# Attention weights times v in 64x64 blocks, with one transpose ahead of them, and a later wait for m

## The chip, the cores and the metric

The kernel runs on one core of one Trainium2 chip. The metric is the device time of one execution in microseconds (us). Engines: TensorE (matmuls, "PE" in the profile, its weight loads "PEld"), VectorE ("DVE"), ScalarE ("ACT"), GpSimd ("POOL") and SyncE ("SP", DMA issues only).

## The reference

One transformer block with adaptive layer norms, for 8 batch rows of 2048 tokens and 256 channels, in 32-bit floats. The attention is linear in the tokens: its scores are a 64x64 matrix per head, from q and k summed over all tokens.

```python
mod = (silu(c) @ wmod)                      # sa, ca, ga, sb, cb, gb of each batch row
h = layernorm(x) * (1 + ca) + sa
q, k, v = split(h @ w_qkv + b_qkv)          # 8 heads of 64
scores = einsum('bhld,bhle->bhde', q, k) / 8
attn = softmax(scores)                      # 64x64 per head
out = einsum('bhld,bhde->bhle', v, attn)
out = layernorm(out @ w_fc + b_fc + h) * gamma + beta
x = x + ga * out
h = layernorm(x) * (1 + cb) + sb            # then a gated FFN on h and h shifted by a token:
x = x + gb * sigmoid(xr @ W_r.T) * (relu(xk @ W_k.T) ** 2 @ W_v.T)
```

## The kernel before

The kernel handles one batch row after another, and each row in four chunks of 512 tokens. It doesn't form q, k and v of the tokens. With z the normalised x of a row (256 channels), it sums the Gram matrix z'z over the row (`turn_and_gram`), puts the weights on both sides of it (`gram_q`, `scores`), takes the softmax of eight 64x64 matrices, and folds attention, the v weights and the output weights into one 256x256 matrix m (`wv_attn`, `make_m`). The attention of a chunk is then z times m (`attention`). Then come the second norm, whose result z2 is transposed (`turn_z2`), and the FFN (`ffn_r`, `ffn_k`, `ffn_out`).

The order of the work is written out by hand, for every engine on its own, and the engines meet in semaphores. `row_steps(b)` of TensorE does the attention and FFN of row b and, between them, the preparation of m for row n = b + 1. It is called for row 0, then by a loop over rows 1 to 6; row 7 has `last_row`, which holds no preparation. So the preparation of m is in seven turns, and once in the start (`wv_attn(0)` and `make_m(0)`), after the constants and weights have been prepared.

The names and lines that matter:

- `wv_attn` (lines 1474 to 1481): four matmuls, one for a pair p of heads. The stationary operand is `attn[:, p]`, 128x128, with the two heads' 64x64 matrices on its diagonal and zeros elsewhere (GpSimd clears it once). The moving operand is `wv_aug[:, p]`, 128 x 256, the v weights. Pairs 0 and 1 go to the PSUM bank att[0], pairs 2 and 3 to att[1]; each bank signals `pv_done` when full. It waits for `attn_ready` (VectorE, line 1087) and `wv_ready` (VectorE, line 1063; in the start GpSimd, line 509).
- ScalarE copies the two banks to SBUF (`copy_pv`, line 642), in two halves, each of which signals `pv_ready`. The copy shares its buffer with gq, so the profile calls it `gq<-att`.
- `make_m` (lines 1483 to 1489): eight matmuls of 256 columns, for each half k of the channels one for each pair p, into the bank gram. It waits for both copies. VectorE then turns the result into m in a high and a low part (lines 1094 to 1099), for which `attention` of the next row waits. In the start `fc_ready` is waited for as well.
- `turn_z2(b, 3)` (lines 1379 to 1393): eight 128x128 transposes of z2 of chunk 3, between `wv_attn` and `make_m`. They wait for z2 (ScalarE, line 717) and for free banks tr. ScalarE's `copy_h2` (line 661) reads them.
- `scores` (lines 1463 to 1472): sixteen matmuls with 128 rows and 64 columns of the stationary operand, head g of a pair in column half g, into partitions 64g to 64g + 63 of the bank gram.
- around them on TensorE, in order: `ffn_out(b, 1)`, `scores(n)`, `ffn_r(b, 2)` (line 1408), `ffn_k(b, 2)` (line 1425), `wv_attn(n)`, `turn_z2(b, 3)`, `make_m(n)`, `ffn_out(b, 2)` (lines 1239 to 1241), then `attention(b + 1, 0)` (the same lines).

Of the kernel before, what the change touches and what calls it, by code (L numbers as in the profile page):

```python
# [30 lines left out]
P = 128  # L31


def adaln_block(nc, x, w_qkv, b_qkv, w_fc, b_fc, gamma, beta, w_r, w_k, w_v, mu_r, mu_k, c, wmod, out):
    B, L, D = x.shape
    HD = w_fc.shape[0]
    DX = 64
    H = HD // DX
    KD = D // P
    NP = H // 2  # L40
    CT = 512
    CH = L // CT
    NT = CT // P
# [10 lines left out]
    with ExitStack() as ctx:  # L54
        def sb(name, shape):
            return ctx.enter_context(nc.sbuf_tensor(name, shape, F32))
# [4 lines left out]
        def bank(name):  # L61
            return ctx.enter_context(nc.psum_tensor(name, [P, 512], F32))

        def sem(name):
            return ctx.enter_context(nc.semaphore(name))
# [3 lines left out]
        tr = [bank(f"tr{h}") for h in range(KD)]  # L69
        att = [bank(f"att{q}") for q in range(2)]  # L70
        work = [bank(f"work{w}") for w in range(3)]

        def r_banks(alone):

            return (att[0], att[1]) if alone else (work[2], work[0])
# [9 lines left out]
        ident = sb("ident", [P, P])  # L85
# [33 lines left out]
        wv_aug = sb("wv_aug", [P, NP, D])  # L119
# [8 lines left out]
        attn = sb("attn", [P, NP, P])  # L128
# [22 lines left out]
        z2 = sb("z2", [P, NT, D])  # L151
# [22 lines left out]
        def mixed(j):  # L174

            return xr[:, j % 2], xk[:, j % 2]
# [58 lines left out]
        wv_ready = sem("wv_ready")  # L235
# [9 lines left out]
        attn_ready = sem("attn_ready")  # L245
        pv_done = sem("pv_done")
        pv_ready = sem("pv_ready")
# [26 lines left out]
        z2_ready = sem("z2_ready")  # L274
        z2_turned = sem("z2_turned")
        h2_ready = sem("h2_ready")
# [20 lines left out]
        def wait_past(eng, semaphore, count):  # L297

            if not isinstance(count, int) or count > 0:
                eng.wait_ge(semaphore, count)  # L300
# [932 lines left out]
        def _(pe):  # L1233
            mm = nc.tensor.matmul
# [87 lines left out]
            def turn_ffn():  # L1322

                pe.wait_ge(ffn_loaded, 48)
                pe.wait_ge(z_lo_ready, 2 * CH)
                pe.wait_ge(row8_b_ready, 1)
                for n, bank in enumerate((tr[0], tr[1], work[0])):
                    for ch in range(KD):
                        for dh in range(KD):
                            ins = nc.tensor.transpose(bank[:, ch * D + dh * P:ch * D + (dh + 1) * P],  # L1330
                                                      w_ffn[:, n, dh, ch * P:(ch + 1) * P], ident[:])
                    ins.then_inc(w_turned, 1)
# [27 lines left out]
            def attention(b, j, alone=False):  # L1360
                i = CH * b + j
                pe.wait_ge(m_ready, b + 1)
                pe.wait_ge(z_lo_ready, 2 * i + 2)
                if not alone:
                    wait_past(pe, t_done, i)
                elif j == 1:
                    pe.wait_ge(h2_ready, 2 * CH * b)
                else:
                    pe.wait_ge(t_done, i - (j == 2))
                for q in range(2):  # L1370
                    for t in (2 * q, 2 * q + 1):
                        tile = slice(t * P, (t + 1) * P)
                        for k in range(KD):
                            ins = mm3(att_banks(j, alone)[q][:, (t % 2) * D:(t % 2 + 1) * D],
                                      (z_hi[:, j, k, tile], z_lo[:, j, k, tile], m_hi[:, k], m_lo[:, k]),
                                      start=(k == 0), stop=(k == KD - 1))
                    ins.then_inc(att_done, 1)

            def turn_z2(b, j, last=False):
                i = CH * b + j  # L1380
                pe.wait_ge(z2_ready, i + 1)


                if last and j == 0:
                    pe.wait_ge(t_done, CH * b + 2)
                elif last or j == CH - 1:
                    wait_past(pe, h2_ready, 2 * i)
                for h in range(KD):
                    if not last and j < CH - 1:
                        pe.wait_ge(z_lo_ready, 2 * (i + 1 + CH) + 1 + h)  # L1390
                    for t in range(NT):
                        ins = nc.tensor.transpose(tr[h][:, t * P:(t + 1) * P], z2[:, t, h * P:(h + 1) * P], ident[:])  # L1392
                    ins.then_inc(z2_turned, 1)

            def ffn_r(b, j, alone=False):

                i = CH * b + j
                pe.wait_ge(xr_mixed, i + 1)
                for q in range(2):
                    if alone:  # L1400
                        pe.wait_ge(t_done, CH * (b + 1))
                        pe.wait_ge(th_ready, 2 * i - 1 + q)
                    elif q == 1:
                        wait_past(pe, ro_ready, 2 * i - 1)
                    for t in (2 * q, 2 * q + 1):
                        tile = slice(t * P, (t + 1) * P)
                        for ch in range(KD):
                            ins = mm(r_banks(alone)[q][:, (t % 2) * D:(t % 2 + 1) * D], mixed(j)[0][:, ch, tile], w_r_t[:, ch],  # L1408
                                     start=(ch == 0), stop=(ch == KD - 1))
                    ins.then_inc(r_done, 1)  # L1410

            def ffn_k(b, j, alone=False):

                i = CH * b + j
                pe.wait_ge(xk_mixed, i + 1)
                for dh in range(KD):
                    if dh == 0 and not alone:
                        wait_past(pe, ro_ready, 2 * i)
                    elif not alone:
                        pe.wait_ge(th_ready, 2 * i + 1)  # L1420
                    elif j == CH - 1:
                        pe.wait_ge(k_lo_ready, 2 * i - 1 + dh)
                    rows_dh = slice(dh * P, (dh + 1) * P)
                    for ch in range(KD):
                        ins = mm(k_banks(alone)[dh][:], w_k_t[:, ch, rows_dh], mixed(j)[1][:, ch],  # L1425
                                 start=(ch == 0), stop=(ch == KD - 1))
                    ins.then_inc(k_done, 1)
# [19 lines left out]
            def turn_gram(b):  # L1447

                pe.wait_ge(g_up_ready, b + 1)
                nc.tensor.transpose(gram[:, D + P:2 * D], g_sb[:, 0, P:D], ident[:]).then_inc(gram_turned, 1)  # L1450
# [21 lines left out]
                ins.then_inc(score_done, 1)  # L1472

            def wv_attn(b):

                pe.wait_ge(attn_ready, b + 1)
                pe.wait_ge(wv_ready, b + 1)
                for p in range(NP):
                    ins = mm(att[p // 2][:, (p % 2) * D:(p % 2 + 1) * D], attn[:, p], wv_aug[:, p], start=True, stop=True)  # L1479
                    if p % 2:  # L1480
                        ins.then_inc(pv_done, 1)

            def make_m(b):

                pe.wait_ge(pv_ready, 2 * b + 2)
                for k in range(KD):
                    for p in range(NP):
                        ins = mm(gram[:, k * D:(k + 1) * D], pv_t[:, p, k * P:(k + 1) * P], wfc_c[:, p], start=(p == 0), stop=(p == NP - 1))  # L1488
                ins.then_inc(m_done, 1)

            def row_steps(b, first):

                n = b + 1
                attention(b, 0)
                turn_and_gram(n, 0)
                if not first:
                    ffn_r(b - 1, 3)
                    ffn_k(b - 1, 3)
                attention(b, 1)
                if not first:  # L1500
                    ffn_out(b - 1, 3)
                turn_and_gram(n, 1)
                turn_z2(b, 0)
                attention(b, 2)
                turn_and_gram(n, 2)
                ffn_r(b, 0)
                ffn_k(b, 0)
                turn_z2(b, 1)
                attention(b, 3)
                ffn_out(b, 0)  # L1510
                turn_and_gram(n, 3)
                turn_z2(b, 2)
                turn_gram(n)
                ffn_r(b, 1)
                ffn_k(b, 1)
                gram_q(n)
                ffn_out(b, 1)
                scores(n)
                ffn_r(b, 2)
                ffn_k(b, 2)  # L1520
                wv_attn(n)
                turn_z2(b, 3)
                make_m(n)
                ffn_out(b, 2)

# [38 lines left out]
            bias_v()  # L1564
            mod_b_columns()
            turn_ffn()
            wv_attn(0)
            pe.wait_ge(fc_ready, 1)
            make_m(0)
            pe.wait_ge(w_copied, 5)  # L1570
            row_steps(0, True)
# [27 lines left out]
```

## Time and profile before

| | us |
|---|---|
| median of 3 runs | 679.94 (679.27 to 681.49) |
| the profiled execution | 681.61 |
| its span | 679.8 |
| TensorE busy | 654.6 |
| VectorE busy | 567.8 |
| ScalarE busy | 457.0 |
| GpSimd busy | 294.0 |
| mean granted clock of TensorE | 0.991 of full |

The profile is of one execution. The span runs from the first instruction to the last; the execution's own time is 1.8 us longer. Matmuls are pipelined and their ends are modelled, so a matmul row's duration is longer than its share of the engine: the distance from one start to the next tells what it costs. A group "x8" lasts from the first start to the last modelled end. "L1479" is line 1479 of the kernel before. A 32-bit matmul appears as two weight loads and two matmul records, here called passes; a transpose appears as one.

### The profile page before, as it was taken

The page shows a single profiled execution, that of the slowest core. Times are in us where ns is not written, and L with a number is a line of the kernel's source. Part 1 is how long each engine was busy: PE and PEld are TensorE (multiplying, and loading weights), DVE is VectorE, ACT ScalarE, POOL GpSimd, SP SyncE. Part 2 cuts the span into 40 slices and gives each one's busy share as a digit, 9 for nine tenths or more (in the row PEclk, how much of TensorE's full clock was granted, in tenths as well). Part 3 has the DMA queues.
Part 4 walks back from the last instruction along what each step waited for, and adds up shares of the span by engine and source line. Part 5 has one row for each costly group of instructions (what it writes and reads, how often), then busy time and mean ns, then how long its engine had stood idle before and what let it go on. Part 6 is the DMA issues. An engine that isn't in the chain of part 4 may idle for free.

```text
span 679.8 us, 12488 instructions
## 1 busy us (share of the span) xinstructions
PE 654.6 (96%) x3968; PEld 535.5 (79%) x3968; DVE 567.8 (84%) x1328; ACT 457.0 (67%) x983; POOL 294.0 (43%) x499
## 2 busy tenths in 40 slices
PE   8978799999999999999999999999999999999896
PEld 6657777889869887889878888798878888697665
DVE  5893988889798897889888897889888897859973
ACT  1423767676966779667867769577776769667662
POOL 5263452764318442574227542383327643215230
PEclk9988999999999999999999999999999999999999
DMA  8859237384854958086765758268673737537325
GB/s 315 224 166 198 89 113 160 61 182 123 195 111 83 230 109 208 31 167 165 162 123 100 170 125 204 79 108 224 129 156 62 128 84 169 101 76 154 63 32 92
DMA packets 90985, 93.04 MB, mean 137 GB/s; under 512 B 4224, under 2 KB 89000, under 8 KB 90960
## 3 DMA queue, kind: packets, MB, share of 16 engines
q0 software_dynamic: 33264, 33.03, 32.9%
q1 hardware_dynamic: 55344, 55.97, 26.1%
q10 hardware_dynamic: 2352, 3.73, 1.5%
q8 instruction: 12, 0.20, 0.1%
q14 instruction: 13, 0.11, 0.0%
HBM read 42.84 MB, written 33.10 MB: 112 GB/s over the span
## 4 chain that ended last, share of the span: by engine, by line
PE 85%; DVE 7%; POOL 2%; ACT 2%; DMA 2%; issue 2%; DVEq 0%; POOLq 0%; ACTq 0%
PE work L1408 14%; PE work L1425 14%; PE gram L1355 10%; PE att L1239 4%; PE work L1239 4%; PE gram L1488 4%; PE work L1240 4%; PE work L1241 4%; PE att L1241 4%; PE att L1240 4%; PE tr L1392 4%; PE att L1460 4%; PE tr L1348 3%; PE att L1479 2%; PE gram L1470 1%
## 5 line engine op out<-in xcount | busy, mean ns | idle before, releaser
L478 POOL TENSOR_TENSOR rs<-ve,neg_half 128x4 f32<-128x4 f32 x32 | 37.4, 1170 | 179.3 <-DVE ve L945 179.3
L1425 PE MATMUL work<-mx,w_k_t 128*128 128x512 f32 x244 | 109.9, 592 | 0.0
L1408 PE MATMUL work<-w_r_t,mx 128*128 128x256 f32 x464 | 106.0, 381 | 0.3 <-DVE mx L983 0.3
L717 ACT ACTIVATE z<-x,nm,rs 128x256 f32<-128x256 f32 x128 | 66.4, 594 | 46.5 <-POOL nm L480 46.5
L1408 PEld LDWEIGHTS work<-w_r_t,mx 128*128 128x128 f32 x464 | 85.8, 190 | 11.8 <-DVE mx L983 0.5
L1355 PE MATMUL gram<-z 128*128 128x256 f32 (+1 forms) x512 | 89.1, 327 | 0.0
L1355 PEld LDWEIGHTS gram<-z 128*128 128x128 f32 x512 | 79.8, 191 | 6.6
L1425 PEld LDWEIGHTS work<-mx,w_k_t 128*128 128x128 f32 x244 | 46.3, 190 | 46.0 <-issue 42.4
L1239 PE MATMUL att<-m_lo,z_hi 128*128 128x256 f32 x248 | 74.9, 302 | 3.8 <-issue 2.0
L1239 PE MATMUL work<-wvf_lo,k_hi 128*128 128x256 f32 x248 | 72.0, 290 | 2.5 <-issue 2.5
L1240 PE MATMUL att<-m_hi,z_hi 128*128 128x256 f32 x248 | 70.8, 285 | 0.0
L1241 PE MATMUL att<-m_hi,z_lo 128*128 128x256 f32 x248 | 70.7, 285 | 0.0
L1241 PE MATMUL work<-wvf_hi,k_lo 128*128 128x256 f32 x248 | 69.1, 279 | 0.0
L1240 PE MATMUL work<-wvf_hi,k_hi 128*128 128x256 f32 x248 | 69.1, 278 | 0.0
L652 ACT ACTIVATE sq<-att 128x256 f32<-128x256 f32 x124 | 45.7, 381 | 33.1 <-PE att L1241 33.1
L924 DVE SCALAR_TENSOR_TENSOR t_buf<-att,rs_o,g_row 128x256 f32<-128x256 f32 x124 | 51.4, 477 | 10.7 <-POOL rs_o L487 9.9
L485 POOL TENSOR_TENSOR ve_o<-ssq,eps_att 128x4 f32<-128x4 f32 x32 | 17.0, 531 | 94.0 <-ACT sq L652 94.0
L661 ACT ACTIVATE h2t<-tr,mod_now 128x512 f32<-128x512 f32 x64 | 46.4, 781 | 15.2 <-PE tr L1392 15.2
L1000 DVE TENSOR_TENSOR k_lo<-work,k_hi 128x512 fp32r<-128x512 f32 x60 | 40.6, 689 | 18.7 <-ACT k_hi L702 18.5
L492 POOL DMA_DIRECT2D x<-in_L_attn_x_dram x32 | 55.2, 1823 | 0.0
L957 DVE SCALAR_TENSOR_TENSOR mx<-h2t,rest_col,mx 128x512 f32<-128x512 f32 x56 | 39.4, 745 | 17.5 <-ACT mx L670 17.5
L1239 PEld LDWEIGHTS att<-m_lo,z_hi 128*128 128x128 f32 x248 | 48.0, 193 | 7.5 <-issue 7.5
(186 smaller groups left out, 1633.1 us busy)
## 6 DMA issues: line engine op xcount, KB each, us to landing
x_in<-in_L_attn_x_dram SPq DMA_DIRECT2D x32, 512.0 KB, 5.1
x<-rows SPq DMA_DIRECT2D x32, 512.0 KB, 3.5
x<-in_L_attn_x_dram POOLq DMA_DIRECT2D x32, 512.0 KB, 8.7
out_dram<-x SPq DMA_DIRECT2D x31, 512.0 KB, 5.3
out_dram<-y POOLq DMA_DIRECT2D x29, 512.0 KB, 5.9
rows<-row_scratch SPq DMA_DIRECT2D x16, 128.0 KB, 5.0
rows<-row_scratch SPq DMA_DIRECT2D x8, 256.0 KB, 4.0
wqkv_sb<-in_L_attn_w_qkv_dram ACTq DMA_DIRECT2D x1, 1536.0 KB, 9.5
```

Of the source, the lines that this page charges most:

```text
L492: nc.gpsimd.dma_start(x2[:, j], x_v[b, j], accum_op=ALU.add).then_inc(x2_filled[j], 16)
L652: ins = nc.scalar.activation(sq[:, t], att_banks(j, alone)[t // 2][:, (t % 2) * D:(t % 2 + 1) * D], ACT.Square, scale=float(D) ** -0.5, ac ...
L661: nc.scalar.activation(h2t[:, h, 1 + j * CT:1 + (j + 1) * CT], tr[h][:], ACT.Identity, bias=mod_now[:, h:h + 1], scale=mod_now[:, 2 + h:3 ...
L717: ins = nc.scalar.activation(z2[:, t], x2[:, j, t], ACT.Identity, bias=nm_2[:, s, t:t + 1], scale=rs_2[:, s, t:t + 1])
L924: ins = nc.vector.scalar_tensor_tensor(t_buf[:, t], att_banks(j, alone)[t // 2][:, (t % 2) * D:(t % 2 + 1) * D], rs_o[:, s, t:t + 1], g_ro ...
L1000: nc.vector.tensor_tensor(lo[:, h], k_banks(alone)[h][:], hi[:, h].bitcast(F32), ALU.subtract).then_inc(k_lo_ready, 1)
L1239: mm(dst, s_hi, m_lo, start=start, stop=False)
L1240: mm(dst, s_hi, m_hi, start=False, stop=False)
L1241: return mm(dst, s_lo, m_hi, start=False, stop=stop)
L1355: ins = mm(gram[:, k * D:(k + 1) * D - k * P], z[:, j % 2, t, k * P:(k + 1) * P], z[:, j % 2, t, k * P:D], start=(j == 0 and t == 0 and k ...
L1408: ins = mm(r_banks(alone)[q][:, (t % 2) * D:(t % 2 + 1) * D], mixed(j)[0][:, ch, tile], w_r_t[:, ch], start=(ch == 0), stop=(ch == KD - 1))
L1425: ins = mm(k_banks(alone)[dh][:], w_k_t[:, ch, rows_dh], mixed(j)[1][:, ch], start=(ch == 0), stop=(ch == KD - 1))
```

## The change

`wv_attn` uses eight matmuls with 64x64 stationary blocks in place of four with 128x128. Head g of pair p is taken from partitions 64g to 64g + 63 of attn and of the v weights, and written to the same partitions of the same bank and columns as before. Its two waits move to its callers. In a turn it is called from a new function, `turn_z2_around_wv`, which waits for everything first, does one of the eight transposes of z2 of chunk 3, then `wv_attn`, then the other seven. `make_m` waits for the first half of the copies at its beginning, and for the second ahead of its third matmul.

```diff
+            def turn_z2_around_wv(b):
+                i = CH * b + CH - 1
+                pe.wait_ge(z2_ready, i + 1)
+                wait_past(pe, h2_ready, 2 * i)
+                pe.wait_ge(attn_ready, b + 2)
+                pe.wait_ge(wv_ready, b + 2)
+                nc.tensor.transpose(tr[0][:, 0:P], z2[:, 0, 0:P], ident[:])
+                wv_attn(b + 1)
+                for h in range(KD):
+                    for t in range(h == 0, NT):
+                        ins = nc.tensor.transpose(tr[h][:, t * P:(t + 1) * P], z2[:, t, h * P:(h + 1) * P], ident[:])
+                    ins.then_inc(z2_turned, 1)
+
@@
             def wv_attn(b):
-
-                pe.wait_ge(attn_ready, b + 1)
-                pe.wait_ge(wv_ready, b + 1)
                 for p in range(NP):
-                    ins = mm(att[p // 2][:, (p % 2) * D:(p % 2 + 1) * D], attn[:, p], wv_aug[:, p], start=True, stop=True)
+                    for g in range(2):
+                        head = slice(g * DX, (g + 1) * DX)
+                        ins = mm(att[p // 2][head, (p % 2) * D:(p % 2 + 1) * D], attn[head, p, head], wv_aug[head, p],
+                                 start=True, stop=True)
                     if p % 2:
                         ins.then_inc(pv_done, 1)
 
             def make_m(b):
 
-                pe.wait_ge(pv_ready, 2 * b + 2)
+                pe.wait_ge(pv_ready, 2 * b + 1)
                 for k in range(KD):
                     for p in range(NP):
+                        if k == 0 and p == 2:
+                            pe.wait_ge(pv_ready, 2 * b + 2)
                         ins = mm(gram[:, k * D:(k + 1) * D], pv_t[:, p, k * P:(k + 1) * P], wfc_c[:, p], start=(p == 0), stop=(p == NP - 1))
                 ins.then_inc(m_done, 1)
 
@@
                 scores(n)
                 ffn_r(b, 2)
                 ffn_k(b, 2)
-                wv_attn(n)
-                turn_z2(b, 3)
+                turn_z2_around_wv(b)
                 make_m(n)
                 ffn_out(b, 2)
 
@@
             turn_ffn()
+            pe.wait_ge(attn_ready, 1)
+            pe.wait_ge(wv_ready, 1)
             wv_attn(0)
             pe.wait_ge(fc_ready, 1)
             make_m(0)
```

## Rows read from the trace of the kernel before

**Rows 1.** The page: busy time with share of the span, chain by engine.

```profile
PE 654.6 (96%) x3968; PEld 535.5 (79%) x3968; DVE 567.8 (84%) x1328; ACT 457.0 (67%) x983; POOL 294.0 (43%) x499
...
PE 85%; DVE 7%; POOL 2%; ACT 2%; DMA 2%; issue 2%; DVEq 0%; POOLq 0%; ACTq 0%
```

**Rows 2.** One turn: length, busy us of PE, PEld, DVE, ACT, POOL, granted clock, DMA.

```profile
165.42:243.59 78.17, 78.16 (x483) 64.69 (x482) 68.78 (x163) 57.71 (x124) 35.88 (x61) 1.00 0.64 142
```

**Rows 3.** The chain in order of time: start us, us on it, what.

```profile
141.93 3.46 PE work L1408 x16
...
204.78 1.73 PE att L1479 x8
...
207.38 3.53 PE gram L1488 x16
...
282.94 1.73 PE att L1479 x8
```

**Rows 4.** Timeline around the block, turn of row 2: start us, us, what.

```profile
204.18 0.59 PE L1425 MATMUL work<-mx,w_k_t 128*128 128x512 f32 x1
204.61 0.38 PE L1479 MATMUL att<-wv_aug,attn 128*128 128x256 f32 x1
...
206.34 1.04 PE L1392 MATMUL tr<-ident,z 128*128 128x128 f32 x8
...
207.21 0.46 PE L1488 MATMUL gram<-wfc_c,gq 128*128 128x256 f32 x1
```

**Rows 5.** Timeline of ScalarE in the same turn.

```profile
199.61 2.07 ACT L717 ACTIVATE z<-x,nm,rs 128x256 f32<-128x256 f32 x4 [5.34 <-POOL nm L480]
...
206.54 0.60 ACT L642 ACTIVATE gq<-att 128x512 f32<-128x512 f32 x1 [0.27 <-PE att L1479]
...
208.76 0.78 ACT L661 ACTIVATE h2t<-tr,mod_now 128x512 f32<-128x512 f32 x1
```

**Rows 6.** Timeline around the scores, same turn, in growing windows.

```profile
193.67 0.60 ACT L633 ACTIVATE gq<-att 128x512 f32<-128x512 f32 x1 [0.46 <-PE att L1460]
196.33 0.28 PE L1241 MATMUL work<-wvf_hi,k_lo 128*128 128x256 f32 x1
...
196.54 0.39 PE L1470 MATMUL gram<-wqk_aug,gq 128*64 128x64 f32 x6
...
196.54 1.15 PE L1470 MATMUL gram<-wqk_aug,gq 128*64 128x64 f32 x32
...
197.62 0.48 PE L1408 MATMUL work<-w_r_t,mx 128*128 128x256 f32 x1
...
201.18 3.60 PE L1425 MATMUL work<-mx,w_k_t 128*128 128x512 f32 x8
```

**Rows 7.** Timeline of VectorE around the block, and the next attention's first matmul.

```profile
203.05 0.85 DVE L1087 TENSOR_TENSOR attn<-s_exp,s_inv 64x256 f32<-64x256 f32 x2
...
212.23 0.71 DVE L1099 TENSOR_TENSOR m_lo<-m_sb,m_hi 128x512 fp32r<-128x512 f32 x1
...
213.58 0.28 PE L1239 MATMUL att<-m_lo,z_hi 128*128 128x256 f32 x1
```

**Rows 8.** The start: timeline, and the granted clock in stretches (after the five engines).

```profile
49.90 3.69 PE L1479 MATMUL att<-wv_aug,attn 128*128 128x256 f32 x8 [2.24 <-POOL wv_aug L509]
...
53.01 0.57 PE L1479 MATMUL att<-wv_aug,attn 128*128 128x256 f32 x1
53.62 0.60 ACT L642 ACTIVATE gq<-att 128x512 f32<-128x512 f32 x1 [1.05 <-PE att L1479]
54.33 0.51 PEld L1488 LDWEIGHTS gram<-wfc_c,gq 128*128 128x128 f32 x3 [1.41 <-issue]
...
50.00:52.00 2.00, 2.00 (x5) 1.64 (x6) 2.00 (x5) 0.02 (x1) 2.00 (x3) 0.50 0.01 1
52.00:54.00 2.00, 1.58 (x4) 0.75 (x3) 0.50 (x3) 0.95 (x2) 2.00 (x3) 0.65 1.01 160
```

**Rows 9.** Behind the start: VectorE's wait for m.

```profile
58.09 0.69 DVE L1094 TENSOR_TENSOR m_sb<-gram,res 128x512 f32<-128x512 f32 x1 [5.59 <-PE gram L1488]
```

## The prediction

> **What bounds the kernel now.** I read the busy shares first [rows 1], then a whole turn of the batch loop [rows 2], then the chain of work that ended last [rows 3], and only then single instructions. TensorE is busy 96% of the span, and the chain runs through it for 85%. VectorE at 84% is the only other engine near. The share alone doesn't decide: the turns do. In a turn of 78.17 us TensorE is busy for 78.16, at full granted clock (2.4 GHz). In the chain the block attention weights times v (line 1479) returns every 78.2 us (204.78, 282.94), and between one block and the next nearly all pieces are TensorE's. So a microsecond that TensorE gains or loses anywhere in a turn moves everything behind it, in this turn and in all later ones: there is no stall in a turn on something that TensorE doesn't itself set. That holds from batch row 1 on. The stretch before it (the start, up to about 84 us) is another regime: TensorE waits there for VectorE and ScalarE, and I cost it apart.
>
> Seven turns (batch rows 0 to 6) hold one such block each, the start holds an eighth. Each matmul in full 32-bit shows as two passes: four matmuls give eight records.
>
> **The block as it is.** The last pass of the matmul with 512 columns starts at 204.18, the eight passes of line 1479 run from 204.61, eight transposes from 206.34, the first pass of m (line 1488) is recorded at 207.21 [rows 4]. So eight passes cost 206.34 - 204.61 = 1.73 us (0.216 each), and eight transposes 0.87 (0.109 each). Then a small stall: m needs both copies of the result (line 642), and the second ends at 206.54 + 0.60 = 207.14 [rows 5], 0.07 before TensorE is through with the transposes. So m's first weight load isn't hidden behind the last transpose. The chain shows what that costs: the sixteen passes of m take 3.53 there, and sixteen passes of the same size take 3.46 at line 1408 in an undisturbed place [rows 3]. The first m record says the same, 0.46 against 0.38 for a pass of line 1479 of the same size [rows 4]. I take 0.08.
>
> **Part 1, the 64x64 blocks.** The four matmuls with a 128x128 stationary operand (two heads on the diagonal, zeros elsewhere) become eight with 64x64: sixteen passes of 256 columns. If the two heads run beside each other, it is again eight passes' time. The trace has no 64-row matmul, so I bound it. The nearest rows are the scores (line 1470): 128 rows by 64 columns, the two heads of a pair in the two column halves of one bank, each written as the new block is, g inside p [rows 6]. Six records end at 196.54 + 0.39 = 196.93 and all 32 at 197.69. Each lasts 0.22, so the sixth starts at 196.71 and the last at 197.47: 26 records in 0.76, that is a pair every 0.0585 us. A pass of 64 columns alone would need 64/256 of 0.216 = 0.054. So the halves do run beside each other, and the pair costs 0.0045 more than a pass. That gives 8 x (0.216 + 0.0045) = 1.77 for the block, +0.04. The ends: below, half of it, 0.86, if a pass in a 64-row tile took half the time (no row speaks for it, and none excludes it); above, 16 x 0.216 = 3.46, if the heads didn't overlap. I take 1.77, since the scores are the one block in this trace that is tiled.
>
> What the tiling costs at its two edges, the scores show too. The pass ahead of them starts at 196.33 and takes 0.12, so the array is free at 196.45. Behind them line 1425 starts at 201.18, and the sixteen passes of line 1408 ahead of it need 3.46, so these stream from 197.72. Between the two lie 1.27 us, of which 16 x 0.0585 = 0.94 are the passes. The other 0.33 are the way in and out, and I take 0.34 for them since the record times are rounded: about 0.14 in (first record 0.09 late, then a load of 64 columns that nothing hides), 0.20 out (line 1408's first record is at 197.62, 0.10 after the last pair has streamed, and its load of 0.11 is bare). It isn't a wait for data: the scores' operands (copies at line 633) were there at 194.27 [rows 6]. The new block lies between transposes on the full array, so it has both edges. No row shows them for 64x64; ends: 0, if only the scores' shape has them, and 0.34. I take 0.34, the row of the one tiled block.
>
> Here a rule of the Trainium skill speaks against the change, TensorEngine Tiling (Array Packing), section Key Properties: changing the tiling mode, as opposed to the tile, drains TensorE. The page gives no time; the trace agrees, with the 0.34 us above. By the rule the edges are paid once per block whatever stands next to it, so the transpose put ahead wouldn't save the first.
>
> **Part 2, one transpose ahead, seven behind.** The number stays. The first needs z2 (ScalarE's line 717 ended at 199.61 + 2.07 = 201.68 [rows 5]), long there at 204.61. The waits for attn and wv move ahead of it: attn is ready at 203.05 + 0.85 = 203.90 [rows 7], also in time. So nothing queued behind those waits (the transposes, m, the output matmuls, the next attention) is held. The block's result comes 0.11 + 0.14 later; its copies then end near 206.45 and 207.45, m later still, and line 661, which reads the transposes, starts only at 208.76 [rows 5]. Cost: 0.
>
> **Part 3, m waits later.** m starts on the first half of the copies and needs the second only for its fifth pass. With seven transposes (0.76) behind the block, TensorE is free near 207.6, so both copies are there: the stall of 0.08 goes. What is late next? m's result goes through VectorE (lines 1094 to 1099) until 212.94, and the attention that needs it starts at 213.58 [rows 7]: 0.64 of slack, and both ends move together.
>
> Sum of a turn: +0.34 + 0.04 - 0.08 = +0.30. Seven turns: **+2.1 us**.
>
> **The start.** Here TensorE had stood still, and its granted clock is 0.50, 1.2 of 2.4 GHz: the eight passes take 0.43 each, from 49.90, the last from 53.01, so it is free at 53.44 [rows 8]. m waits for the second copy (53.62 + 0.60 = 54.22) and its first weight load is at 54.33, streaming from 54.44. The granted clock is on its way up by then (0.65 over 52 to 54), and I take it as full for m. With the change the block ends 0.04 later, the way out costs 0.20, and m streams from 53.68: its first four passes reach 54.54, and the second copy is there at about 54.36. So m ends 0.76 earlier. What follows is VectorE, which was idle for 5.59 us before m came [rows 9], then attention, ScalarE and VectorE again; nothing on that way comes from elsewhere as far as I see, so I let the 0.76 through. Ends: 0 (some transfer or the clock takes it back) and -0.76.
>
> **Sum.** 7 x 0.30 - 0.76 = +1.34 us. The profiled execution took 681.61 (span 679.8), so this is 682.95 on its scale. The median of the three runs is 679.94, 1.67 below it; I put the change on the median: **681.3 us**, +0.20%.
>
> **The rivals.**
> A, slower: the two heads don't overlap. They lie in different row halves, which the scores never do, and write one bank. Then each turn has eight passes more, 8 x 0.216 = 1.73, seven times, 12.1, and the start 8 x 0.43 = 3.4: 681.3 + 15.5 = 696.8. For it: no row has a row tile. Against it: the column halves share a bank in the scores and overlap in full. It decides early: 0.3% is 2.04 us, about what a measurement can tell from no change, and only 0.10 us a turn above my sum reaches it, half of one pass without a partner. One whole pass alone at each block's end gives 683.2.
> The Trainium skill has this as a rule, TensorEngine Tiling (Array Packing), Gotcha 1: different row tiles cannot access the same PSUM bank at the same time. The change puts both heads of a pair in one bank, in different partitions; if the rule held regardless of partitions, the time would be that of rival A. No row here shows a row tile.
> B, no edges: the edges belong to the scores' shape, or are hidden. 681.3 - 7 x 0.34 - 0.2 = 678.7, within 0.3%. Against it: both edges are bare in rows, on an engine with no wait for data.
> C, faster: a pass in a 64-row tile takes half. 0.86 less than 1.73 a turn, 7 x 0.86 = 6.0, and the start 1.7: 673.6. The scores can't refute it, as their passes might be held by the load of 64 columns instead of the stream.
> D, the start gives nothing back: 682.1, within my case.
>
> **How the numbers follow.** My case, both edges with full overlap: 0.67, at 681.3, own range 680.2 to 683.8 (lower end: edges at two thirds; upper end: one pass alone at each block, 683.2, and D in part). A 0.12, B 0.13, C 0.08. The range takes in my case and B and leaves out A and C: 678.3 to 684.0, 0.80. Faster by over 0.3% (below 677.9): C and a little, 0.09. Slower (above 682.0): A, and some two fifths of my case, 0.38. Within 0.3%: the rest, 0.53.
>
> **What would show it.** Line 1479's successor should have 16 records a block, in pairs that start within 0.01 us of each other and 0.22 apart; single records 0.22 apart over 3.4 us mean A; pairs 0.11 apart mean C. The first record after the one transpose should be late by 0.09 or more, and the first of the seven behind it too; if neither is, B. The sixteen passes of m should take 3.46. Blocks should return every 78.47 us against 78.17. In the start, m should begin near 53.6. I would be wrong above all if the tiles of 64 rows behave unlike those of 64 columns, since every term but two is read from the latter.

## The result

The changed kernel takes 681.25 us (median of 17 runs, 679.92 to 683.09), the kernel before in the same measurements 679.36. The ratio is 1.0021, with a 95% interval of 1.0011 to 1.0030: slower by 0.7 to 2.0 us, 1.4 in the middle, while the medians differ by 1.9. That is within 0.3%, and next to the forecast 681.3. An execution over 1.5% slower than the fastest of its kernel is left out of the ratios; there were two in all, of 1356 and 1923 us. The parts of the sum fared less well than the sum, as the experiments show.

The profiled execution took 681.60 us, its span is 679.7. The page of the changed kernel: busy times, the granted clock in 40 slices, the chain by engine.

```profile
PE 658.5 (97%) x4032; PEld 533.9 (79%) x4032; DVE 567.8 (84%) x1328; ACT 456.9 (67%) x983; POOL 292.9 (43%) x499
...
PEclk9988999999999999999999999999999999999899
...
PE 86%; DVE 7%; DMA 3%; ACT 2%; POOL 1%; issue 1%; DVEq 0%; POOLq 0%; ACTq 0%
```

TensorE has 64 records more (eight blocks, eight passes more in each) and stays what bounds the kernel, as in [rows 1]. Line numbers have moved: wv_attn is line 1491 (1479 before), m is 1503 (1488), the first transpose 1401, the seven 1405, ffn_r 1421, ffn_k 1438.

The chain in the turn of row 2, and the same block in the last turn (start us, us on the chain, what):

```profile
203.50 0.11 PE tr L1401
203.60 1.87 PE att L1491 x16
205.48 0.91 PE tr L1405 x7
206.39 3.46 PE gram L1503 x16
...
595.08 1.87 PE att L1491 x16
```

The answer to [rows 3]: block and transposes took 1.73 + 0.87 = 2.60 there and take 0.11 + 1.87 + 0.91 = 2.89 here, m goes from 3.53 to 3.46. Six turns pass from the block of row 1's preparation at 125.39 to 595.08, so a turn takes 78.28.

The timeline of the same block, in windows that grow:

```profile
203.33 0.27 PE L1401 MATMUL tr<-ident,z 128*128 128x128 f32 x1
203.53 0.43 PE L1491 MATMUL att<-wv_aug,attn 64*64 64x256 f32 x2
...
203.53 0.65 PE L1491 MATMUL att<-wv_aug,attn 64*64 64x256 f32 x4
...
203.53 1.94 PE L1491 MATMUL att<-wv_aug,attn 64*64 64x256 f32 x16
205.41 0.33 PE L1405 MATMUL tr<-ident,z 128*128 128x128 f32 x1
205.41 0.44 PE L1405 MATMUL tr<-ident,z 128*128 128x128 f32 x2
...
206.23 3.62 PE L1503 MATMUL gram<-wfc_c,gq 128*128 128x256 f32 x16
```

Two passes start within a window of 0.02 us, and the next two within another at 203.80: they start in pairs. A record of this form lasts 0.376 (the first two, which wait for their weights, 0.427). Four records end at 203.53 + 0.65 = 204.18, so the fourth starts at 203.80; all sixteen end at 205.47, so the last starts at 205.10. Between the two lie six pairs, 0.216 each. That is the distance of single passes before, so the two heads overlap in full and rival A is out; and since a pair takes a full pass's time, not half of it, C is out too. The transpose ahead starts at 203.33 and needs 0.109, so the first pair is due at 203.44; it is recorded at 203.53 and, reckoned back from the second pair, streams from 203.59. The last pair has streamed at 205.31; the next transpose is recorded at 205.41 and its successor 0.165 later, where 0.109 is usual. These are the edges: 0.15 in, 0.15 out. Rival B is out as well.

### The profile page after: what moved, and what is told of

It is laid out like the page before. It is cut to its first block, busy times and chain, and to the rows that moved or that the text cites. A ratio compares the mean times of both kernels' runs of the same rounds, so it can differ in the third digit from the quotient of the medians.

```text
span 679.7 us, 12622 instructions
## 1 busy us (share of the span) xinstructions
PE 658.5 (97%) x4032; PEld 533.9 (79%) x4032; DVE 567.8 (84%) x1328; ACT 456.9 (67%) x983; POOL 292.9 (43%) x499
## 4 chain that ended last, share of the span: by engine, by line
PE 86%; DVE 7%; DMA 3%; ACT 2%; POOL 1%; issue 1%; DVEq 0%; POOLq 0%; ACTq 0%
PE work L1438 15%; PE work L1421 14%; PE gram L1355 10%; PE work L1239 4%; PE gram L1503 4%; PE work L1241 4%; PE work L1240 4%; PE att L1239 4%; PE att L1240 4%; PE att L1241 4%; PE att L1473 4%; PE tr L1348 3%; PE tr L1392 3%; PE att L1491 2%; PE att L1421 2%; DMA rows<-row_scratch 2%
## 5 line engine op out<-in xcount | busy, mean ns | idle before, releaser
L1355 PE MATMUL gram<-z 128*128 128x256 f32 (+1 forms) x512 | 90.7, 331 | 0.0
```

Of the source, the lines that this page charges most:

```text
L1355: ins = mm(gram[:, k * D:(k + 1) * D - k * P], z[:, j % 2, t, k * P:(k + 1) * P], z[:, j % 2, t, k * P:D], start=(j == 0 and t == 0 and k ...
```

## The experiments

Each comparison ran on one chip beside the kernel before; "us" in what follows is the ratio's interval times 680.

### The order and the later wait without the tiles

```diff
-                    for g in range(2):
-                        head = slice(g * DX, (g + 1) * DX)
-                        ins = mm(att[p // 2][head, ...], attn[head, p, head], wv_aug[head, p], ...)
+                    ins = mm(att[p // 2][:, ...], attn[:, p], wv_aug[:, p], ...)
```

> The changed kernel, but with four matmuls of 128x128 in place of eight of 64x64: the order and the later wait alone. My theory: the tiling costs its two edges in each turn (0.147 in and 0.151 out in the changed kernel's trace) and gives nothing back, and the later wait is worth 0.08 for the stall ahead of m and 0.09 for ffn_out(b, 2), whose passes then come 0.113 apart in place of 0.118. So this one should be faster than before by 7 x 0.17 = 1.2 us and by 1.0 in the start: -2.2 us, ratio near 0.997, turns of 78.00 us. Rival: the edges are not what costs, something else in the changed kernel does, and this one is as slow as the changed kernel, +1.9 us.

Measured: 679.54 against 679.71, ratio 0.9993 (0.9982 to 1.0004), -0.5 us (-1.2 to +0.3). A turn takes 78.03:

```profile
125.14 1.73 PE att L1489 x8
...
593.30 1.73 PE att L1489 x8
```

(593.30 - 125.14) / 6 = 78.03, 0.25 less than with the tiles. So the tiles are what costs; the rival is out, since this kernel isn't as slow as the changed one. But I expected -2.2, and the interval holds no change. The turn is right (78.00 expected), so what failed is the start's -1.0, and the pace of ffn_out(b, 2), which stays at 0.118 in some turns.

### The later wait alone

```diff
-                pe.wait_ge(pv_ready, 2 * b + 2)
+                pe.wait_ge(pv_ready, 2 * b + 1)
                 for k in range(KD):
                     for p in range(NP):
+                        if k == 0 and p == 2:
+                            pe.wait_ge(pv_ready, 2 * b + 2)
```

> The kernel before, with nothing changed but the wait for the second half of the copies, which m makes ahead of its third matmul. My theory: all that the change gives comes from this wait, so it is as fast as the one with the order as well, -2.2 us against before, with turns of 78.00 us. Rival: the transpose put ahead is needed (TensorE would still come to m before the first copy, or its queue would run dry there), and this one stays within 0.5 us of before.

Measured: 679.13, ratio 0.9984 (0.9974 to 0.9994), -1.1 us (-1.8 to -0.4). The chain of a turn, where m follows eight transposes at once:

```profile
204.10 1.73 PE att L1479 x8
205.83 0.87 PE tr L1392 x8
206.71 3.46 PE gram L1490 x16
```

m takes 3.46 in place of 3.53 [rows 3] and needs no transpose ahead for it. Its turns take 78.03, as in the kernel with the order as well, so with full blocks the transpose ahead isn't needed and gives nothing. This kernel has the lowest median of the study and is the only one clear of no change on the fast side. Three other kernels hold the same wait without tiles, the one above and two of those with fillers, and aren't clear of no change (-0.5, -0.1 and -0.3 us), so -1.1 is likely more than it is worth. The size is half of what I expected, for the same two reasons.

### Tiles and order with the early wait

```diff
-                pe.wait_ge(pv_ready, 2 * b + 1)
+                pe.wait_ge(pv_ready, 2 * b + 2)
@@
-                        if k == 0 and p == 2:
-                            pe.wait_ge(pv_ready, 2 * b + 2)
```

> The changed kernel with m waiting for both copies at its beginning, as before: the blocks of 64x64 and the order alone. My theory: in each turn the wait costs 0.05 ahead of m and 0.09 in ffn_out(b, 2), whose passes go back to 0.118, so 7 x 0.14 = 1.0, and the start loses its gain of about 0.8: 1.8 us above the changed kernel, +3.7 us against before. Rival: the wait is hidden by the seven transposes and the pace of ffn_out has another cause: then only the start's 0.8 comes on top, +2.7 us, and ffn_out(b, 2) keeps 0.113.

Measured: 682.86, ratio 1.0039 (1.0025 to 1.0054), +2.6 us (+1.7 to +3.7). The chain in a turn:

```profile
204.30 1.87 PE att L1491 x16
206.17 0.91 PE tr L1405 x7
207.08 3.51 PE gram L1501 x16
```

m takes 3.51, so the wait still costs 0.05 behind seven transposes, as my theory had it. A turn takes 78.37, 0.09 above the changed kernel, where I expected 0.14. The total meets the rival's +2.7 and not my +3.7, but the rival's reason, a wait hidden by the transposes, doesn't hold. For the start this profile settles nothing: from the block's first record to m's it is 2.82 us here and 2.82 in the changed kernel, but the clock was up sooner here (granted 0.79 from 50 to 52, against 0.51), and m did stand 0.79 us for its second copy.

### The tiling left and entered once more

```diff
-                wv_attn(b + 1)
+                wv_attn(b + 1, between=lambda: nc.tensor.transpose(tr[0][:, P:2 * P], z2[:, 1, 0:P], ident[:]))
                 for h in range(KD):
-                    for t in range(h == 0, NT):
+                    for t in range(2 * (h == 0), NT):
```

Here `wv_attn` calls `between` behind pair 1.

> The changed kernel with one of the seven transposes moved into the middle of the block, between pairs 1 and 2, in the turns: the same work, but the tiling is left and entered once more. My theory: each way in costs 0.15 and each way out 0.15, so a turn is 0.30 longer, 7 x 0.30 = 2.1 us above the changed kernel, +4.0 against before. Rival: the cost belongs to the first tiled pass after a long full-size matmul or to the weights' first load, not to the switch; then a second switch costs nothing, and this one equals the changed kernel.

Measured: 683.53, ratio 1.0044 (1.0032 to 1.0057), +3.0 us (+2.2 to +3.9). The timeline of the block:

```profile
204.81 0.27 PE L1401 MATMUL tr<-ident,z 128*128 128x128 f32 x1
205.01 1.08 PE L1491 MATMUL att<-wv_aug,attn 64*64 64x256 f32 x8
206.02 0.33 PE L1402 MATMUL tr<-ident,z 128*128 128x128 f32 x1
206.28 1.08 PE L1491 MATMUL att<-wv_aug,attn 64*64 64x256 f32 x8
207.29 0.88 PE L1405 MATMUL tr<-ident,z 128*128 128x128 f32 x6
208.00 1.25 PE L1505 MATMUL gram<-wfc_c,gq 128*128 128x256 f32 x5
```

From the first transpose to m's first record it takes 208.00 - 204.81 = 3.19 us, in the changed kernel 206.23 - 203.33 = 2.90: 0.29 more (0.30 unrounded) for the same passes. The turn goes from 78.28 to 78.60; by the ratios the distance is 3.0 - 1.4 = 1.6 us, where I expected 2.1 and the turns give 2.2. So the edges are paid at each switch, 0.30 for a way in and a way out, and the rival is out. The Trainium skill's rule (TensorEngine Tiling (Array Packing), Key Properties: a change of the tiling mode drains TensorE) agrees with it.

### The kernel before once more

Nothing is changed.

> The kernel before itself, once more, for a second profile of it and for what two equal kernels differ by in one measurement. Both theories expect a ratio whose interval holds 1.000 and turns of 78.17 us. What is open is the start: the first scores of the second turn begin at 118.37 in the first profile of before. If the start is the same in each execution, they begin within 0.2 us of that here; if it wanders (as five kernels of this study let one think: 116.8 to 118.1), they may be up to 1.5 us off, and a comparison of two single profiles can't tell what the change did to the start.

Measured: ratio 1.0002 (0.9991 to 1.0012); the medians of the two equal kernels differ by 0.5. The start does wander: these scores, which lie in the turn of row 0 and ahead of its block, begin at 119.76, against 118.37. Nearly all of it is there at the block's first record already, 51.27 against 49.90 [rows 8]. The turns wander too, which I hadn't expected: this profile has turns of 78.17 and 78.00 in alternation, and 78.09 on the mean. And both profiled executions of before were slow ones of their kind: 681.61 where the median is 679.36, 682.51 where it is 680.48. The one of the changed kernel was 0.35 above its median.

### The start alone, and the turns alone

The first has the new `wv_attn(0)` and `make_m(0)` in the start and the old ones in the turns; the second the reverse:

```diff
             pe.wait_ge(wv_ready, 1)
-            wv_attn(0)
+            for p in range(NP):
+                ins = mm(att[p // 2][:, ...], attn[:, p], wv_aug[:, p], start=True, stop=True)
+                if p % 2:
+                    ins.then_inc(pv_done, 1)
             pe.wait_ge(fc_ready, 1)
+            pe.wait_ge(pv_ready, 2)
             make_m(0)
```

> The kernel before, with the blocks of 64x64 and the later wait in the start alone; the turns are as before. My prediction's term: -0.76 us (ratio 0.9989). Rival, from the sums of the four runs so far, where the turns' part taken off the measured difference leaves between -0.2 and +1.0 for the start: the gain ahead of m is taken back before the turns begin, by the clock or by a transfer that ends when it did, and this kernel is as fast as before or up to 0.5 us slower.

> The changed kernel, with the start as before (blocks of 128x128, m waits for both copies there). My prediction's term: 7 x 0.30 = +2.1 us. From the traces since then I expect less: the block up to m's end costs 0.22 a turn, and the passes of the output and attention matmuls give back up to 0.1 of it, so turns of 78.28 and +0.8 to +1.6 us. Rival: the start's part is nil, and this one shows the changed kernel's whole +1.9 us.

Measured: the start alone 680.03 against 679.99, ratio 0.9998 (0.9987 to 1.0008), -0.1 us (-0.9 to +0.5). The turns alone 681.89, ratio 1.0027 (1.0011 to 1.0042), +1.8 us (+0.7 to +2.9), with turns of 78.25 in its profile. The forecast's two terms, -0.76 and +2.1, both lie inside; so do a start worth nothing and turns worth +1.1. Timing alone doesn't part them.

### The heads apart

```diff
-                for p in range(NP):
-                    for g in range(2):
-                        head = slice(g * DX, (g + 1) * DX)
+                for q in range(2):
+                    for g in range(2):
+                        head = slice(g * DX, (g + 1) * DX)
+                        for p in (2 * q, 2 * q + 1):
...
```

> The changed kernel, with the two heads' matmuls not in turn: in each bank first both of head 0 (four passes), then both of head 1. If each 64x64 tile works off its own passes as soon as they are in TensorE's window, as the pairs that start 0.007 apart let one think (the program has two passes of head 0, then two of head 1, and still they start in pairs), the sixteen passes stay eight pairs and the block takes 1.73 us. Rival: a pass can't start ahead of one that stands before it in the program; then per bank only the last pass of one head and the first of the other meet, and the block takes about 13 x 0.216 = 2.8 us, 1.1 more a turn.

One execution: 682.63, of which the time alone says little. The timeline of the block:

```profile
204.15 0.27 PE L1401 MATMUL tr<-ident,z 128*128 128x128 f32 x1
204.36 1.99 PE L1492 MATMUL att<-wv_aug,attn 64*64 64x256 f32 x16
206.28 0.98 PE L1405 MATMUL tr<-ident,z 128*128 128x128 f32 x7
```

The block is 1.92 long (206.28 - 204.36) where it is 1.88 in the changed kernel (205.41 - 203.53), not 2.8. The passes still start in pairs, 0.216 from pair to pair, though the program has four of one head, then four of the other; within a pair they start 0.013 us apart in the first bank and up to 0.058 in the second, where the changed kernel has 0.007. The records don't say which head a pass belongs to, but in program order the sixteen would have needed the rival's 2.8. So each tile works off its own passes, and a pass can start ahead of one that stands before it.

### Fillers for the clock in the start

`warm(n, bank)` makes n transposes of the identity into a bank that is free there; the fourth kernel has ten more ahead of `turn_z2(b, 2)` in the last row.

```diff
+            pe.wait_ge(s_dif_ready, 1)
+            pe.wait_ge(gq_ready, 2)
+            warm(10, att[0])
             wv_attn(0)
@@
             pe.wait_ge(w_copied, 5)
+            warm(16, tr[0])
             row_steps(0, True)
```

> The kernel before, with 10 transposes of the identity into a free bank ahead of the start's block and 16 ahead of the first attention, where TensorE stands still for 2.2 and 2.0 us; nothing else. My theory: in the start TensorE works at 1.2 GHz because of these two standstills (granted clock 0.50 from 48 to 52, 0.55 to 0.59 from 60 to 64), and its passes there are on the way to the first turn. With them filled, the second stretch runs at full clock, 24 passes at 0.118 in place of 0.213, and the first rises 1 us or more earlier: 1.5 to 3 us faster than before. Rival: what ends last in the start is a transfer or VectorE, and the clock doesn't matter: as fast as before, or slower by what the fillers delay.

> The changed kernel with the same fillers. My theory: with the start's clock the same in both, this one against the one before with fillers shows the change's own effect: 7 turns of +0.15 to +0.22 in place of the +0.30 that I forecast, and in the start the later wait's gain less the way out of the tiling, about -0.5: +0.5 to +1.1 us over before with fillers. Rival: the start gives nothing even so, and the distance is +1.5 to +2.0.

> The kernel before with the later wait and the same fillers, no tiles, no transpose ahead. My theory: 7 x 0.08 from the stall and about 0.7 in the start over before with fillers, -1.3 us; against before without them -3 to -4 us. Rival: the later wait is worth the turns' 0.5 us and nothing in the start.

> The same as the third, with 10 more filler transposes in the last batch row, where TensorE waits 1.4 us for z2 of chunk 2 and the clock fell in the changed kernel's profile (0.88 from 640 to 650). My theory: the clock falls there in some executions only, so the median gains 0 to 0.5 us more. Rival: the fillers come late for the wait and cost up to 0.3.

Measured, against the kernel before: before with fillers 1.0013 (0.9990 to 1.0035); changed with fillers 1.0024 (1.0015 to 1.0034); later wait with fillers 0.9998 (0.9986 to 1.0011); the same with fillers in the last row 0.9995 (0.9984 to 1.0005). No filler paid, and my expectation of 1.5 to 3 us failed. The first ratio holds one execution of 688.79 us with a granted clock of 0.96; without it the mean is about 0.1 us above the kernel before's. The changed kernel lies 682.08 - 680.56 = 1.5 us above the one before, both with fillers, in the medians: more than the +0.5 to +1.1 that I expected, and as much as the rival's +1.5. The later wait lies 0.8 below it, where I expected 1.3, and ten more fillers in the last row moved nothing (679.77 against 679.78).

What these kernels do show is what else can hold the start. The chain of the changed kernel with fillers:

```profile
51.63 3.66 PE gram L1503 x16
...
57.22 7.80 DMA rows<-row_scratch
...
66.54 1.58 DVE t_buf L924 x4
```

m's records begin at 51.56, 2.8 us ahead of [rows 8], and m is done in both parts at 57.20; and still VectorE's t_buf for chunk 0 comes at 66.5. Ahead of it VectorE stands at line 1039, the preparation of the next batch row. That waits for a row of 256 modulation values, spread over all partitions (128 KB), whose load SyncE may only issue when m is ready, and that load takes 7.80. In the kernel before, the same load takes 4.3 and isn't last. VectorE and the issues, kernel before first, then the changed kernel, then the changed one with fillers:

```profile
49.71 5.47 POOL L492 DMA_DIRECT2D x<-in_L_attn_x_dram  x4
60.00 0.33 SPq L312 DMA_DIRECT2D rows<-row_scratch  x1
64.29 0.15 DVE L1039 TENSOR_SCALAR neg_d<-rows 128x1 f32<-128x1 f32 x1 [4.04 <-DMA rows<-row_scratch]
```

```profile
64.54 0.15 DVE L1039 TENSOR_SCALAR neg_d<-rows 128x1 f32<-128x1 f32 x1 [5.78 <-DMA rows<-row_scratch]
```

```profile
65.12 0.15 DVE L1039 TENSOR_SCALAR neg_d<-rows 128x1 f32<-128x1 f32 x1 [7.64 <-DMA rows<-row_scratch]
```

Issued at 60.0, 58.5 or 57.2, the row is there at 64.3, 64.5 and 65.1: never before 63.8 in fourteen profiles. What it lies behind is in the traces: GpSimd's four loads of 512 KB, issued from 49.71. In the changed kernel the row is issued at 58.50, and from there to 62 only GpSimd's queue (q0) moves anything (packets, MB, share of the 16 DMA engines' time):

```profile
q0 software_dynamic: 691, 0.69, 123.9%
```

SyncE's queue (q1), with the row in front, has its first packet at 62.57, and GpSimd's last one ends at 64.16. It is so in all fourteen profiles: wherever the row was issued, from 57.2 to 61.4, its first packet comes at 62.2 to 64.3, no more than 2.7 us ahead of the end of GpSimd's loads, and VectorE has the row 0.2 to 0.9 behind that end. So GpSimd's loads set when the row comes, not the time at which m is ready. A kernel that holds them back was not tried.

And where TensorE came early to that wait, it lost the clock behind it (two stretches of the changed kernel with fillers; the granted clock is the third figure from the end):

```profile
65.00:70.00 5.00, 1.75 (x8) 1.78 (x9) 4.81 (x11) 2.99 (x4) 0.00 (x0) 0.65 0.50 175
70.00:75.00 5.00, 5.00 (x31) 4.95 (x31) 4.10 (x18) 2.18 (x10) 1.56 (x4) 0.66 0.30 107
```

TensorE had stood still for 4.4 us up to 68.25, for t_buf and so for this row, and the next 24 passes of attention came 0.21 apart, those of 1.2 GHz. In the two kernels with the later wait and fillers the clock fell too, behind 1.9 and 3.6 us. Not so in the kernel before with fillers, whose second slow stretch is gone:

```profile
55.00:60.00 5.00, 4.78 (x31) 4.13 (x30) 1.88 (x4) 0.00 (x0) 0.00 (x0) 1.00 1.23 194
60.00:65.00 5.00, 5.00 (x39) 4.90 (x40) 0.92 (x5) 2.67 (x11) 0.83 (x2) 1.00 1.13 219
```

Its profile reaches the scores at 116.82, earlier than both profiles of the kernel before, and still its median isn't lower. So the fillers removed the slow stretch in one kernel and moved it in three, and paid in neither case. The first slow stretch they couldn't reach: in the kernel before the granted clock is 0.78 from 46 to 47 already, ahead of the standstill that I had blamed for it (47.7 to 49.9).

## Why the prediction was right or wrong

**What bounds the kernel** held: TensorE's blocks set the turn, and 0.3 us added in a turn (the edges twice) came out as 0.32.

**The passes.** The heads overlap, as taken from the scores. A pair costs 0.216, not 0.2205, so the term +0.04 is 0. The second rule of the Trainium skill that I weighed (TensorEngine Tiling (Array Packing), Gotcha 1: no two row tiles in the same PSUM bank at once) doesn't hold here: passes of two row tiles start 0.007 us apart in one bank, in different partitions. The measurement decides. Row tiles that write the same partitions were not tried.

**The edges.** Forecast 0.34, measured 0.298: 0.147 in, as in the scores, and 0.151 out, not 0.20. What lies behind the block is a transpose, and its bare weight load shows as 0.056 (0.165 against 0.109), where line 1408's in the scores shows as 0.10. I had priced the way out by a successor of another kind.

**The transpose ahead** cost and gave nothing, nor did the moved waits, where the blocks are full: the turns take 78.03 with them and without (the first two experiments). The tiles without that transpose were not tried.

**The later wait.** Forecast -0.08, measured -0.07: m's sixteen passes in 3.46, from 3.53. With the wait early again, 0.05 returns.

So the block up to m's end costs +0.22, not +0.30. **The turn** got less than that: 78.28 against 78.17 in the first profile of before and 78.09 on the mean in the second, +0.11 to +0.19. The rest is in the attention and output matmuls, whose passes (lines 1239 to 1241) come 0.113, 0.118 or 0.120 apart. In the changed kernel's turn of row 2, most of ffn_out(b, 2) is at 0.113, as these lines of its chain show; in the kernel before it is at 0.118, and at 0.113 in other stretches.

```profile
210.20 0.11 PE work L1239
210.32 0.11 PE work L1240
210.43 0.11 PE work L1241
```

I first put this on the later wait; the later wait alone and the full blocks showed both paces in their turns, and so did two profiles of one and the same kernel. What sets the pace stays open. It moves a turn by up to 0.17. Over all profiles the distance is steadier: 78.25 to 78.28 in the three with tiles and later wait in the turns (the changed kernel, the turns alone, with fillers), 78.09 to 78.16 in the four with the old turns, +0.15 on the means.

**Seven turns** are then +0.8 to +1.3 in the profiles, where +2.1 was forecast; measured alone +1.8 (+0.7 to +2.9). In two of the profiles with tiles something comes on top: the clock falls in the last batch row (from 640 to 650 granted 0.88 in the changed kernel, 0.83 in the turns alone; below the changed kernel, then the kernel before):

```profile
640.00:650.00 10.00, 10.00 (x47) 7.55 (x45) 9.79 (x24) 5.01 (x10) 2.54 (x2) 0.88 0.01 2
```

```profile
640.00:650.00 10.00, 9.32 (x47) 6.53 (x45) 9.79 (x23) 4.85 (x10) 2.54 (x2) 1.00 0.00 0
```

From the last turn's scores to the end the changed kernel's profile needs 92.94, the kernel before's 92.46: 0.26 more than the block's own 0.22. But that isn't the clock's price: the changed kernel with fillers needs 92.97 there at full clock, and the turns alone, with the deeper fall, 92.77. The four other profiles with tiles in the turns show 1.00 there, so the fall belongs to no tile; whether a later arrival makes it likelier isn't shown.

Six turns and this end together are then 6 x 0.15 + 0.38 = +1.3 us on the means of these profiles, an estimate that leaves the start out. The ratio's +1.4 (0.7 to 2.0) leaves -0.6 to +0.7 for the start, so -0.76 just not.

**The start** is the step that most likely failed. Forecast -0.76, let through to the median. The gain itself is in the traces: from the block's first record to m's there are 4.46, 4.53 and 4.24 us in the three profiles with the old start (the kernel before twice, and the turns alone), 3.47 in the start alone and 3.31 in the later wait alone, so nearly all of it is the later wait. The changed kernel has 2.82, but there the clock also came back sooner (granted 1.00 from 52 to 54, against 0.65 in [rows 8]), which the start alone, with the same start, doesn't show (0.50). And in the start alone the gain goes on: from the block to the scores it is 67.66 us, against 68.47, 68.49 and 68.29, 0.6 to 0.8 less. What the profiles can't show is whether it counts in a usual execution, since the block's own first record wanders by more (49.90 to 51.27 in the kernels without fillers). The changed kernel's start, m's first record and the chain behind it:

```profile
50.02 2.89 PE att L1491 x16
52.91 3.67 PE gram L1503 x16
58.50 5.94 DMA rows<-row_scratch
65.87 1.66 DVE t_buf L924 x4
```

By the timings the start alone gives -0.1 (-0.9 to +0.5): no gain seen, -0.76 just inside. I had let the gain through since "nothing on that way comes from elsewhere": the load of the row does. In the changed kernel it is there at 64.54, and t_buf starts 1.33 later, at 65.87, and that distance is the same in all six profiles where the row comes last (1.33 or 1.34). That is still 1.43 earlier than the 67.30 of the kernel before's profile, where the row (64.29) isn't last. But I had put the gain on the median although it was read from an execution 1.7 above it. An estimate for the median itself: its span of 677.6, less 92.5 for the end, 6 x 78.12 for the turns and the 51.1 from t_buf to the scores, puts its t_buf at about 65.3, and so the row at about 63.9 or before, next to the earliest of fourteen profiles (63.84). In such an execution the row would be last already, and an earlier m would gain nothing; that is rival D's case. No profile was taken of one, so this isn't shown.

So 681.3 was met in part by luck, through two errors of opposite sign: the turns cost less in the trace than forecast (+1.3 with the end, against +2.1), the start gave less in the timings (about 0, against -0.76). How much less each, within some 0.7 us, these runs don't settle. The mechanism of the turns (heads side by side, two edges, the later wait) was right.

## What to carry to other kernels

A block-diagonal operand already does both heads in one pass: a single pass and a pair of 64x64 passes both took 0.216 us. So here the tiling could only add its two edges, 0.15 us in and 0.15 out, each time the array is switched. On an engine that is busy all through, look first for a wait on several pieces of data that could be a wait on the first of them: that alone gave the lowest median here, and turns 0.06 to 0.14 us shorter. And take no gain in a start-up stretch from one profile: find the transfer that ends next and what it queues behind, take a second profile of the unchanged kernel, which here differed from the first by 1.4 us, and ask whether the profiled execution is a usual one.

## What the runs showed of the hardware that I had not expected

Passes to different 64x64 tiles don't keep the program's order among each other: with four passes of one head ahead of four of the other, the sixteen still took eight pairs' time (1.92 against 1.88 us). The passes of 256 columns in the reduced 32-bit format come 0.113, 0.118 or 0.120 us apart at full clock, and which it is changes from turn to turn in one and the same kernel, so that equal turns differ by 0.17 us of 78. A load of 128 KB that SyncE issued waited until GpSimd's 2 MB were nearly through, in all fourteen profiles, so that issuing it 1.5 us earlier (at 58.50 and not 60.00) brought it no earlier (64.54 against 64.29). And the granted clock was at half in one or two stretches of the start between 43 and 74 us, the later ones behind standstills of 1.9 to 4.4 us; in the last row, behind 1.3 and 0.8 us of standstill, it fell in two profiles and not in the eleven others that have the same waits. Where fillers removed the later stretch, the kernel was no faster.
